# Fetching table rows by one-hot matrix products: the table as three bf16 parts in place of fp32

## The reference

```python
seg = lambda v: jax.ops.segment_sum(v, dst, num_segments=n)
xs = x[src]
deg_w = jnp.maximum(seg(edge_weights), 1.0)
deg_c = jnp.maximum(seg(jnp.ones_like(edge_weights)), 1.0)
norm = edge_weights / jnp.sqrt(deg_w[src] * deg_w[dst])
gcn = seg(norm[:, None] * xs) @ Wgcn + bgcn
sage = x @ Wsage_s + seg(xs) / deg_c[:, None] @ Wsage_n + bsage
agg_w = seg(edge_weights[:, None] * xs)
gin = ((1.0 + gin_eps) * x + agg_w) @ Wgin + bgin
gconv = x @ Wgc1 + agg_w @ Wgc2 + bgc
eop = seg(edge_weights[:, None] * jax.nn.relu(xs + edge_attr)) @ Wedge + bedge
```

## Time and profile before

| | us |
|---|---|
| three runs | 2219.24, 2228.43, 2227.15 (median 2227.15) |
| profiled execution | 2228.75 |
| its span, first to last instruction | 2226.9 |
| PE busy | 1556.4 (70%), 6037 products |
| POOL busy | 1355.2 (61%) |
| DVE busy | 928.6 (42%) |
| ACT busy | 826.9 (37%) |

### The profile page before, as it was taken

One profiled execution on the slowest core, in us unless ns is written; L12 is line 12 of the kernel. 1 busy time (PEld: TensorE's weight loads), 2 busy tenths in 40 slices (PEclk: granted clock), 3 DMA queues, 4 the chain that ended last, 5 costly groups with the idle time before them and its releaser, 6 DMA issues.

```text
span 2226.9 us, 22565 instructions
## 1 busy us (share of the span) xinstructions
PE 1556.4 (70%) x6037; PEld 1007.5 (45%) x6037; DVE 928.6 (42%) x2539; ACT 826.9 (37%) x1201; POOL 1355.2 (61%) x1426
## 2 busy tenths in 40 slices
PE   1004367566888777877878778777887888877876
PEld 1003367553554544544445445444444445544546
DVE  5684256543433332433433433243333334423346
ACT  1676233243433433424244234233333324423323
POOL 7665366556666656656666666566666656665660
PEclk9999967688989888978889888888888888888988
DMA  5111234331222222222222222222222222222223
GB/s 98 23 24 51 70 100 112 95 80 42 51 64 45 55 54 46 57 46 44 54 57 53 47 57 43 47 58 50 48 66 43 48 51 57 47 53 44 59 55 77
DMA packets 83186, 126.12 MB, mean 57 GB/s; under 512 B 29494, under 2 KB 31269, under 8 KB 82821
## 3 DMA queue, kind: packets, MB, share of 16 engines
q0 software_dynamic: 45056, 48.85, 13.6%
q1 hardware_dynamic: 36371, 74.90, 11.0%
q10 hardware_dynamic: 1650, 1.04, 0.2%
HBM read 121.29 MB, written 3.40 MB: 56 GB/s over the span
## 4 chain that ended last, share of the span: by engine, by line
PE 43%; issue 18%; another core or an unknown queue 17%; DVE 10%; ACT 4%; POOL 3%; DVEq 2%; DMA 1%; SPq 0%; POOLq 0%; ACTq 0%
PE psum L1280 27%; PE psum L1261 13%; ACT ring L604 4%; POOL ring L559 3%; DVE ring L1076 2%; DVE sums L1065 2%; DVE early L988 1%; PE psum L1312 1%; PE psum L1228 1%; DVE attr L953 1%; DVE early L992 1%; DMA ring<-node_table,idx 1%; PE psum L1341 1%; PE psum L1342 1%
## 5 line engine op out<-in xcount | busy, mean ns | idle before, releaser
L559 POOL DMA_INDIRECT ring<-node_table,idx x1280 | 1228.4, 960 | 758.2 <-issue 389.4
L1280 PE MATMUL psum<-table_sb,early_x 128*128 128x455 f32 x2240 | 988.1, 586 | 115.6 <-issue 110.1
L1280 PEld LDWEIGHTS psum<-table_sb,early_x 128*128 128x128 f32 x2240 | 446.0, 205 | 573.4 <-issue 566.7
L1261 PE MATMUL psum<-ring 128*128 128x120 f32 x2560 | 405.3, 313 | 246.5 <-issue 127.5
L1261 PEld LDWEIGHTS psum<-ring 128*128 128x128 f32 x2560 | 375.5, 224 | 310.2 <-issue 164.9
L988 DVE TENSOR_TENSOR early<-psum,digit_hot 128x455 f32<-128x455 f32 x160 | 100.6, 631 | 989.5 <-remote 599.3
L688 ACT ACTIVATE early_x<-early,minus_ids 128x256 f32<-128x256 f16 x560 | 370.4, 744 | 138.7 <-remote 103.4
L655 ACT ACTIVATE ring<-attr 128x512 f32<-128x512 f32 x160 | 100.2, 626 | 483.4 <-DVE attr L953 383.8
L679 ACT ACTIVATE early<-early 128x256 f32<-128x256 f32 x40 | 16.7, 416 | 518.2 <-DVE early L1009 385.1
L1065 DVE TENSOR_TENSOR sums<-sums,psum 64x40 f32 (+1 forms) x648 | 127.5, 197 | 97.4 <-remote 53.6
L526 POOL DMA_INDIRECT early_x<-in_x,early_idx x128 | 122.0, 953 | 61.4 <-issue 40.3
(11 more groups left out here) (158 smaller groups left out, 644.8 us busy)
## 6 DMA issues: line engine op xcount, KB each, us to landing
attr<-in_edge_attr SPq DMA_DIRECT2D x79, 512.0 KB
ring<-node_table,idx POOLq DMA_INDIRECT x1280
early<-in_edge_attr SPq DMA_DIRECT2D x36, 256.0 KB
src_all<-in_src SPq DMA_DIRECT2D x16, 512.0 KB
early<-key_rows SPq DMA_DIRECT2D x10, 512.0 KB
early_x<-degree_rows SPq DMA_DIRECT2D x2, 1568.0 KB
early_x<-in_x,early_idx POOLq DMA_INDIRECT x128
node_table<-table_sb SPq DMA_DIRECT2D x1, 1666.0 KB, 6.0
```

The costliest lines, as they stand in the source:

```text
L559: nc.gpsimd.indirect_dma_start(out=feat[:, u, j, D:BLOCK], out_offset=None, in_=table, in_offset=bass.IndirectOffsetOnAxis(ap=idx[:, u, j: ...
L1261: last = nc.tensor.matmul(to[:, 0:3 * WINDOW], features[:, j, 0:2 * D], hots[:, j].rearrange("p k n -> p (k n)"), start=(j == 0), stop=(j ...
L1280: last = nc.tensor.matmul(pick_ps[k % 2].rearrange("p (b c) -> p b c", b=SPLIT), node_hot[:, k, a], table_sb[:, a * SPLIT:(a + 1) * SPLIT, ...
```

## The change

The table in on-chip memory is split into three bf16 parts whose sum is the fp32 number. The first is a view: the upper half word of each fp32 number, read with a step of two half words. DVE subtracts it from the table into `x_rest` (fp32); the second part is the upper half word of that, again a view; DVE subtracts it into `x_low`, which is bf16 and dense. These two subtractions run on four pieces of the table (14, 14, 14 and 7 tiles), one after each of the four slots of the last early step. The one-hots become bf16. Each product of `pick_tile` becomes three, one for each part, with the same one-hot, all added in the same PSUM bank, and PE waits for `low_ready` in addition. The places in `early_flat` move so that `x_rest`, `x_low` and `node_hot` fit. Nothing else changes.

```diff
-        HOT = SPLIT * P
+        COLS = D + 1
+        at_rest = HEAD * TILES * D
+        at_low = at_rest + NT * COLS
+        at_hots = at_low + -(-NT * COLS // 2)
+        HOT = SPLIT * P // 2
...
+        node_hot = early_flat[:, at_hots:at_hots + HALF * HOT].bitcast(BF16).rearrange(
             "p (k a e) -> p k a e", k=HALF, a=SPLIT)
+        def upper_halves(t):
+            return t.bitcast(BF16).rearrange("p (t c two) -> p t c two", t=NT, two=2)[:, :, 0:COLS, 1]
+        x_rest_flat = early_flat[:, at_rest:at_low]
+        x_rest = x_rest_flat.rearrange("p (t c) -> p t c", c=COLS)
+        x_high = upper_halves(table_sb[:, :, :].rearrange("p t c -> p (t c)"))
+        x_mid = upper_halves(x_rest_flat)
+        x_low = early_flat[:, at_low:at_hots].bitcast(BF16)[:, 0:NT * COLS].rearrange("p (t c) -> p t c", c=COLS)
...
+                def split_table(k):
+                    tiles = pieces[k]
+                    nc.vector.tensor_tensor(out=x_rest[:, tiles], in0=table_sb[:, tiles, 0:COLS], in1=x_high[:, tiles],
+                                            op=ALU.subtract).then_inc(rest_ready, 1)
+                    dve.wait_ge(rest_ready, v * PIECES + k + 1)
+                    nc.vector.tensor_tensor(out=x_low[:, tiles], in0=x_rest[:, tiles], in1=x_mid[:, tiles],
+                                            op=ALU.subtract).then_inc(low_ready, 1)
...
                         if u < chunks:
                             early_features(c)
+                        if splitting:
+                            split_table(u)
...
+                    pe.wait_ge(low_ready, (v + 1) * PIECES)
...
+                    parts = (x_high, x_mid, x_low)
                     for a in range(SPLIT):
-                        last = nc.tensor.matmul(pick_ps[k % 2].rearrange("p (b c) -> p b c", b=SPLIT), node_hot[:, k, a],
-                                                table_sb[:, a * SPLIT:(a + 1) * SPLIT, 0:D + 1],
-                                                start=a == 0, stop=a == SPLIT - 1)
+                        for n_part, part in enumerate(parts):
+                            last = nc.tensor.matmul(pick_ps[k % 2].rearrange("p (b c) -> p b c", b=SPLIT), node_hot[:, k, a],
+                                                    part[:, a * SPLIT:(a + 1) * SPLIT],
+                                                    start=(a, n_part) == (0, 0), stop=(a, n_part) == (SPLIT - 1, len(parts) - 1))
```

More of the change, by code:

```diff
@@ L193, in build @@
         digit_hot = sb("digit_hot", [P, PICKED * TILES, SPLIT], BF16)
-        HOT = SPLIT * P
-        at_hots = HEAD * TILES * D
-        assert at_hots + HALF * HOT <= EARLY * TILES * D
-        node_hot = early_flat[:, at_hots:at_hots + HALF * HOT].rearrange(
-            "p (k a e) -> p k a e", k=HALF, a=SPLIT)
+        COLS = D + 1
[3 more added lines that the diff above has]
+        HOT = SPLIT * P // 2
+        assert at_hots + HALF * HOT <= EARLY * TILES * D and at_hots <= (EARLY - UNROLL + 1) * TILES * D and at_low <= (EARLY - UNROLL) * TILES * D
+        node_hot = early_flat[:, at_hots:at_hots + HALF * HOT].bitcast(BF16).rearrange(
+            "p (k a e) -> p k a e", k=HALF, a=SPLIT)
+        def upper_halves(t):
[5 more added lines that the diff above has]
+        x_low = early_flat[:, at_low:at_hots].bitcast(BF16)[:, 0:NT * COLS].rearrange("p (t c) -> p t c", c=COLS)
+        PIECES = UNROLL
+        pieces = [slice(k * 2 * SPLIT, min((k + 1) * 2 * SPLIT, NT)) for k in range(PIECES)]
+        assert pieces[-1].stop == NT
         root_src = sb("root_src", [P, TILES])
@@ L316, in build @@
         key_bias_set, key_row_step = sem("key_bias_set"), sem("key_row_step")
+        rest_ready, low_ready = sem("rest_ready"), sem("low_ready")
         node_far, node_hot_made, picked = sem("node_far"), sem("node_hot_made"), sem("picked")
@@ L961, in weigh_hots, with early_step @@
                     weigh(hot[:, u], 2, wroot[:, u]).then_inc(hots_ready, 1)
-                def early_step(i, begun=True, chunks=UNROLL):
+                def split_table(k):
[5 more added lines that the diff above has]
+                                            op=ALU.subtract).then_inc(low_ready, 1)
+                def early_step(i, begun=True, chunks=UNROLL, splitting=False):
                     firsts = first_windows(dve, BASE - LAG + i * UNROLL, UNROLL)
@@ L1114, in _ @@
                     early_step(i)
-                early_step(EARLY_STEPS - 1)
+                early_step(EARLY_STEPS - 1, splitting=True)
                 turn(0, begun=False)
```

## The result

The changed kernel takes 2262.41 us (median of 4 runs, 2252.81 to 2267.96) against 2227.79 us before (4 runs, 2219.24 to 2240.29): 1.0146 times as long, 95% interval 1.0084 to 1.0209. It is slower, as forecast, but by 35 us and not by 130. The profiled execution took 2252.81 us, 24 us over the one of before.

A forecast was written before the change was run, and what follows sets the result against it. PE's supply of instructions while POOL gathers was taken to bound the kernel. 2228.75 us profiled + 126 for added instructions + 3 for DVE's split = 2358 us; own range 2310 to 2430, with rivals 2110 to 2480.

The forecast's parts named there:

- The budget: PE's instruction supply: after POOL resumes, about 128 instructions at full pace, then about 1.6 a microsecond until POOL pauses.
- Array time: PE's picked tiles: 0.19 us a bf16 product, 4.0 us a tile instead of 5.35, 3.1 us less a pair, hidden.
- Rival 3: PE's stepped bf16 views read slowly, 0.38 us a product: 3 to 4.8 us more a pair, 2440 to 2565 us; chance 0.12.
- rival 1: PE's array time decides and instructions cost nothing: each pair loses 3.1 us, 2012 us; chance 0.17.
- 20 us of gathering: PE during POOL's 16 gathers: 128 instructions in about 12 us, 13 in the next 8 us, 141 of 169.
- Rival 2: PE's starvation begins by time, 16 us after POOL resumes, after some 156 instructions: 2145 us; chance 0.13.
- 28 are left for the pause where six were left: PE instructions of a pair left for POOL's pause: 1.75 to 3.2 us instead of 0.4 to 0.7.
- the pair grows by 1.3 to 2.5 us: Each pair of slots in the turns lengthens, taken as +1.8 us; over 70 pairs +126 us, 91 to 175.
- DVE's split: Subtractions in the last early step, 8.5 to 12.4 us in four slots, partly hidden: 0 to 12.4 us, taken as +3.
- Rival 4: Gain and loss of 1.3 us cancel in pairs where POOL pauses after 10 us: 2217 to 2240 us; chance 0.08.
- The other signs: Changed profile: POOL's pause over 3.4 us, PE busy less in a longer span, granted clock below 0.86 in the turns.
- The sign against it: Forecast wrong if a 20 us stretch of gathering shows 165 or more instructions, or the pair is below 24 us.

The follow-up runs named there:

- g1: Changed kernel with the third part's product left out, 14 products and 14 loads a tile: 2218.92 us beside a kernel before at 2227.41, ratio 0.9974.
- g2: Kernel before (fp32) with the first four of a tile's seven products cut in two by columns: 2261.86 us beside a kernel before at 2227.41, ratio 1.0152.
- j1: Changed kernel multiplying only the first part, x_high, 7 products and 7 loads a tile: 2169.09 us beside a kernel before at 2207.48, one run.
- e: Set of runs: columns cut, two parts, one part (1832.49 to 1833.01 us) and half the gathers (1565.45 us); the kernel before took 1831 us.
- f: Set of runs: kernel before again (1831.54 us), changed kernel again (1831.56), and changed kernel with the third part's product over 7 columns (1829.73).
- h: Set of repeated runs: one part 1830.07 us, half the gathers 1565.45 beforehand and 1565.46 here, narrow third part 1830.88; kernel before at 1830 us.
- i: Set of repeated runs: changed kernel with one part 1834.03 us, kernel before with half the gathers 1565.13 us; the kernel before took 1831 us.
- g: Set of runs: changed kernel with two parts 2218.92 us, kernel before with products cut by columns 2261.86 us; kernel before at 2227.41 us.
- j: Set of runs: changed kernel with one part 2169.09 us, kernel before with half the gathers 1619.62 us; kernel before at 2207.48 us.
- j2: Kernel before with four of a late chunk's eight gathers left out: 1619.62 us beside a kernel before at 2207.48 us, one run.
- f1: Kernel before, unchanged, run against itself with a profile: 1831.54 us, ratio 1.0001.
- f2: Changed kernel, unchanged, run again beside the kernel before: 1831.56 us, ratio 1.0007.

## Why the forecast was too high

1. **What bounds the kernel: right. The budget: right as a count, too simple as a size.** In 20 us stretches the first gap comes after 119 instructions (before), 124 (changed), 121 (g1), 126 (g2) and 115 (j1) on average, at 16.1, 11.7, 12.4, 12.5 and 15.2 us. With rows 7 alone it was a guess that it counts instructions; g1, g2 and the table of pairs bear it out. But in the six 30 us stretches of the changed kernel it comes after 143, in the four of g2 after 150, and j1 starves with 105 a pair. What the budget consists of stays open (below).
2. **Array time: right.** 0.20 us a product for 0.19, 4.24 us a tile for 4.0. Rival 3 falls by the rows at 582 us, rival 1 by g1. The rule on four-byte steps that the prediction sets against rival 3 held for its size, not to the last per cent: the stepped parts take 0.203 and 0.211 us beside 0.192. The saving bought gaps.
3. **20 us of gathering: right.** Forecast were 141 instructions with a failure after 12 us; it was 137, after 11.7. Rival 2 (16 us, over 150) falls.
4. **The failed step: "28 are left for the pause where six were left", and with it "the pair grows by 1.3 to 2.5 us".** 14 fell into it on average, against 9 before, and the pause behind a 20 us stretch did not grow: 3.80 us against 3.77, where +1.8 was forecast. I took each pair for a cycle that must finish its own 169 instructions before POOL goes on. But POOL goes on once the one late chunk it waits for is done, and PE carries its lag through the ring's four slots. It made it up in the stretches that followed at full pace, above all those of 10 us: 96 + 26 instructions in one and its pause, where it was 66 + 22, so the free capacity was there before and unused. g2 does 94 in such a stretch with its array time uncut, so it is not the saved array time that makes room for them. What the change costs shows in the pauses behind the 10 and 30 us stretches, 2.8 and 6.6 us where they were 2.3 and 5.4. With this the 32 instructions a pair cost 0.53 us (24.24 to 24.77) where 1.8 were forecast: 0.53 x 70 = 37 us of the 126, and 35 were measured. That the lag is carried in the ring is read from these counts; no run changed the ring's depth. The prediction read its budget from the 20 and 30 us stretches; its one row of 10 us is from ahead of the turns, so this room was not in its view. Its own sum for the kernel before, 23.3 to 23.7 us for a measured 24.3, was not closed either.
5. **DVE's split: nothing, forecast +3.** DVE is busy 8.2 us more on the page, within the bounds. The first tile starts at 477.8 us, where before it was 479.3.
6. **ACT: right at 0.** L691's 1788 ns are 1788 for bf16 too (L708).
7. **Rival 4** (gain and loss cancel in pairs in which POOL pauses after 10 us) fails: the loss is clear of zero. That the saved array time earns something back in those stretches is not shown. g2 saves none and costs 0.71 us for its 36 instructions more a pair, 0.020 each; the changed kernel costs 0.53 for 31, 0.017 each. That difference is 5 us of the whole, less than the runs spread (2253 to 2268 us).
8. **The other signs** mostly came as listed: the mean pause 3.5 us (over 3.4, but from 3.3), the granted clock 0.79 in the turns, PE busy less in a longer span, and a pair not below 24 us. The sign against it, a 20 us stretch with 165 or more, showed in two of 45 (174 and 175, at 479 and 623 us, in the turns); the other 43 stay below it, and the mean is 137. So the budget is no hard number in each single stretch (standard deviation 12.5).
9. **Not considered:** that the same programs run at 1831 us elsewhere, with no gap. The trace of before could not show it. It did show that DVE has such gaps too (last section).

## What to carry to other kernels

When an engine has "issue" gaps with nothing to wait for, count the instructions since the last pause before you shorten any of them: here halving the array time of the tiles at an equal count gave 0.3%, and more instructions at an equal array time cost 1.5%. A loss inside one period is not a loss of the period while a ring carries the lag and later stretches have room: sum over a few periods, of both kinds. Of what was run, the cheapest thing on PE is fewer, not faster, products (one part, 2169 us beside 2207, with the fetched rows cut to their upper half words), and the strongest is less gathering on POOL (1620 us with half of it left out, which leaves out half of the rows as well).

## What the runs showed of the hardware

- The same program takes 1831 us in four of the six sets of runs (e, f, h, i) and 2227 and 2207 us in the other two (g, j); in the first measurement it took 2228. The record of f, h and j names the same chip by its number, with the kernel before at 1830 and 1830 us and then at 2207. If that number means one part, the condition comes and goes on it; that it does wasn't tested.
- The shortage is not PE's alone. While POOL gathers the rows of the early chunks (its first pause after 20 us is at 81), DVE works through 80 operations of one line (L877; L894 where the table is split). Between them it has gaps of 0.3 to 2.0 us with nothing to wait for, 21 to 23 us in all, in every trace taken where the kernel before takes 2207 us or more (before, after, g1, g2, j1, j2) and in none of the others. In the pages of the kernel before, at 2229 us and at 1834 (f1):

```profile
L877 DVE SCALAR_TENSOR_TENSOR early<-attr,scratch,psum 128x1024 bf16<-128x1024 f32 x80 | 98.1, 1275 | 24.2 <-issue 22.6
...
L877 DVE SCALAR_TENSOR_TENSOR early<-attr,scratch,psum 128x1024 bf16<-128x1024 f32 x80 | 96.2, 1271 | 0.0
```

- The gaps are not the loading of code blocks. With one part the loop's code is short, and the instruction queue q8 moves 20 packets (14 in the turns) where the kernel before moved 53. From 1070 to 2095 us it moves none, and in that time PE has 123 gaps (over 0.3 us, in the middle of a tile or late chunk), 165 us in all. The other queue of that kind, q14, moves 40 to 43 packets from 460 to 2150 us whether PE starves or not. In j1 the "issue" idle time of its late chunks and tiles is 386.8 + 181.6 us. The page of j1:

```profile
q8 instruction: 20, 0.33, 0.1%
...
L1289 PE MATMUL psum<-ring 128*128 128x120 f32 x2560 | 485.0, 348 | 642.0 <-issue 386.8
...
L1311 PE MATMUL psum<-table_sb,early_x 128*128 128x455 bf16 x1120 | 358.5, 455 | 194.4 <-issue 181.6
```

  The Trainium skill (Runtime: NRT & Kernel Launch, Instruction fetch mechanics) calls the fetch mostly hidden; in the 1831 us runs it was, and with no packet in those 1025 us it can't be what shows here. What PE and DVE run out of while POOL gathers stays open.
- A bf16 operand with a step of four bytes is read by PE almost at the pace of a dense one: 0.203 and 0.211 us for 455 columns beside 0.192, and the same in f2 to 0.001.
